# Matmul chains issued in turns into two PSUM banks, in an fp32r attention and MLP kernel

## The reference, cut to what matters

```
for layer in (1, 2):
    h = layer_norm(x)
    q, k, v = h @ wq + bq, ctx @ wk + bk, ctx @ wv + bv      # 16 heads of 128
    k, v = concat(k, bias_k), concat(v, bias_v)              # one more key
    x = x + softmax(q @ k.T / sqrt(128)) @ v @ wo + bo
x = x + gelu(layer_norm(x) @ w_fc1 + b_fc1) @ w_fc2 + b_fc2  # width 2048
```

## Time and profile before

| | us |
|---|---|
| median of 3 runs (lowest, highest) | 2818.55 (2814.38, 2820.99) |
| profiled execution: span from the first to the last instruction | 2818.2 |
| PE busy | 2611.6 (93%) |
| PE weight loads busy | 2209.9 |
| DVE busy | 1351.1 (48%) |
| POOL busy | 910.3 (32%) |
| ACT busy | 889.7 (32%) |
| chain that ended last: PE | 79% of the span |
| of it, matmuls of line 433 | 61% |
| matmuls, and as many weight loads | 14528 |

### The profile page before, as it was taken

One profiled execution on the slowest core, in us unless ns is written; L12 is line 12 of the kernel. 1 busy time (PEld: TensorE's weight loads), 2 busy tenths in 40 slices (PEclk: granted clock), 3 DMA queues, 4 the chain that ended last, 5 costly groups with the idle time before them and its releaser, 6 DMA issues.

```text
span 2818.2 us, 40994 instructions
## 1 busy us (share of the span) xinstructions
PE 2611.6 (93%) x14528; PEld 2209.9 (78%) x14528; DVE 1351.1 (48%) x2100; ACT 889.7 (32%) x2807; POOL 910.3 (32%) x1004
## 2 busy tenths in 40 slices
PE   7998799999899999889979987999998999998898
PEld 5776688888788888767757666888886888887677
DVE  5657633333634334464466576334336333335544
ACT  5775222222222222211147752222223222222110
POOL 4545422322323223232145453223223232233221
PEclk9999899999999999999989998999999999999999
DMA  4000111011111011111130002011011010111100
GB/s 160 23 8 16 64 38 37 32 50 38 57 38 52 30 37 47 40 33 35 64 125 23 8 16 71 31 37 52 30 38 64 30 52 30 37 52 35 37 30 30
DMA packets 34829, 121.70 MB, mean 43 GB/s; under 512 B 3488, under 2 KB 3744, under 8 KB 33696
## 3 DMA queue, kind: packets, MB, share of 16 engines
q1 hardware_dynamic: 34720, 120.27, 12.1%
HBM read 116.06 MB, written 4.19 MB: 43 GB/s over the span
## 4 chain that ended last, share of the span: by engine, by line
PE 79%; issue 7%; DVE 5%; POOL 5%; ACT 2%; DMA 2%; SPq 0%; DVEq 0%; POOLq 0%; ACTq 0%
PE PS L433 61%; PE PS L627 4%; PE PS L609 4%; PE PS L500 3%; PE PS L479 2%; PE PS L618 2%; PE PS L488 2%; POOL X L302 2%; DMA BO<-in_bo_rows 1%; ACT KZ L764 1%; POOL XN L317 1%; DVE XN L1025 1%; PE PS L523 1%; DVE X L967 1%; DVE HF L1043 1%
## 5 line engine op out<-in xcount | busy, mean ns | idle before, releaser
L433 PE MATMUL PS<-AT,W 128*128 128x512 f32 x2496 | 601.0, 392 | 17.7 <-DVE HF L1043 12.1
L433 PEld LDWEIGHTS PS<-AT,W 128*128 128x128 f32 x2496 | 471.6, 189 | 119.5 <-issue 12.5
L967 DVE TENSOR_TENSOR X<-PS,X 128x512 f32<-128x512 f32 x416 | 284.6, 690 | 357.2 <-PE PS L433 352.7
L433 PE MATMUL PS<-CT,W 128*128 128x512 f32 x1728 | 441.0, 404 | 2.9 <-DVE HF L1043 2.9
L433 PE MATMUL PS<-W,CT 128*128 128x256 f32 (+1 forms) x3264 | 421.5, 291 | 19.7 <-DVE CT L917 12.5
L374 POOL TENSOR_TENSOR PR<-PR,RC 128x512 f32<-128x512 f32 x128 | 133.5, 1043 | 935.5 <-DVE RC L1134 935.5
L433 PEld LDWEIGHTS PS<-W,CT 128*128 128x128 f32 x3264 | 410.6, 199 | 20.7 <-issue 12.4
L433 PE MATMUL PS<-W,CX 128*128 128x512 f32 x1584 | 386.8, 399 | 1.5 <-DVE X L967 1.5
L433 PEld LDWEIGHTS PS<-CT,W 128*128 128x128 f32 x1728 | 318.5, 190 | 72.1 <-issue 10.2
L433 PEld LDWEIGHTS PS<-W,CX 128*128 128x128 f32 x1584 | 292.4, 188 | 69.0 <-DVE X L967 3.2
L289 POOL TENSOR_TENSOR W<-RAW,W 128x1024 fp32r<-128x1024 f32 (+1 forms) x136 | 328.6, 2416 | 11.4
(11 more groups left out here) (90 smaller groups left out, 2989.4 us busy)
## 6 DMA issues: line engine op xcount, KB each, us to landing
RAW<-in_wq SPq DMA_DIRECT2D x44, 512.0 KB, 3.3
RAW<-in_wk SPq DMA_DIRECT2D x44, 512.0 KB, 4.2
RAW<-in_wo SPq DMA_DIRECT2D x44, 512.0 KB, 3.3
RAW<-in_wv SPq DMA_DIRECT2D x40, 512.0 KB, 3.3
X<-in_x SPq DMA_DIRECT2D x2, 2048.0 KB, 10.2
BVR<-in_bv_rows SPq DMA_DIRECT2D x8, 512.0 KB, 4.1
BIASVR<-in_biasv_rows SPq DMA_DIRECT2D x8, 512.0 KB, 5.8
out<-X SPq DMA_DIRECT2D x4, 1024.0 KB, 4.3
```

The lines of the kernel that those rows point to most:

```text
L433: ins = nc.tensor.matmul(out, lhs(c, a), rhs(c, b), start=(k == 0), stop=(k == total - 1))
L967: V_.tensor_tensor(X[:, tile, :], PS[:, bank, :], X[:, tile, :], ALU.add).then_inc(done, 1)
```

## The change

Where a chain does not have to wait for its moving operand chunk by chunk (fresh), two chains are issued in turns: one matmul of the first, one of the second. This is done for keys and queries of a head, for the values of a block (a tile of bank BC with a tile of bank BD) and for the two column blocks of hidden(m). The waits of both chains stand ahead of the pair, and both semaphores are raised by the last two matmuls. The number, the shapes and the operands of the matmuls stay as they are, and the other engines' programs are untouched. Chains stay one behind the other for head 0 of a layer's first two blocks and for hidden(0) and hidden(2) of a half's first pair.

```diff
+            def two_chains(first, second, chunks):
+
+                k, total = 0, chunks * len(PASSES)
+                for c in range(chunks):
+                    for a, b in PASSES:
+                        flags = dict(start=(k == 0), stop=(k == total - 1))
+                        one = nc.tensor.matmul(first[0], first[1](c, a), first[2](c, b), **flags)
+                        two = nc.tensor.matmul(second[0], second[1](c, a), second[2](c, b), **flags)
+                        k += 1
+                return one, two
...
                     def qk(n, tb, h, slab, fresh=None):
                         pe.wait_ge(k_ev, n * 2 + h)
-                        keys(n, tb, h, slab)
+                        if fresh is not None:
+                            keys(n, tb, h, slab)
+                            pe.wait_ge(q_ev, n * 2 + h)
+                            queries(n, tb, h, slab, fresh)
+                            return
                         pe.wait_ge(q_ev, n * 2 + h)
-                        queries(n, tb, h, slab, fresh)
+                        if h == 0:
+                            pe.wait_ge(w_ready[1], slab + 1)
+                            pe.wait_ge(w_ready[0], slab + 1)
+                        k_last, q_last = two_chains((PS[:, BB, :], slab_of(1, h * P), block_of(CT, tb)),
+                                                    (PS[:, BA, :], slab_of(0, h * P), block_of(AT, tb)), C)
+                        k_last.then_inc(k_ps, 1)
+                        q_last.then_inc(q_ps, 1)
 
                     def values(n, tb, slab, first):
...
+                        if first == "layer":
+                            pe.wait_ge(xadd, x_count(hf, n) - 2)
+                        elif not first:
+                            pe.wait_ge(xadd, x_count(hf, n) - 4)
...
+                        for b in range(2):
+                            ends = two_chains(tokens(0, b), tokens(1, b), C)
+                        for ins in ends:
                             ins.then_inc(v_ps, 1)
...
+                        if first and e == 0:
+                            for f in range(2):
+                                if m:
+                                    pe.wait_ge(gelu_done, m0 * 2 + (2 * m + f - 1))
+                                fresh = norm_index(hf, LAYERS) * 8 + tb * C if f == 0 else None
+                                project(BA + f, e, 256, f * P, AT, tb, h_ps, fresh)
+                            return
+                        if m:
+                            pe.wait_ge(gelu_done, m0 * 2 + 2 * m)
+                        elif not first:
+                            pe.wait_ge(gelu_done, m0 * 2)
+                        ends = two_chains((PS[:, BA, :], slab_of(e, 0), block_of(AT, tb)),
+                                          (PS[:, BB, :], slab_of(e, P), block_of(AT, tb)), C)
+                        for ins in ends:
+                            ins.then_inc(h_ps, 1)
```

More of the change, by code:

```diff
@@ L441, in project, with slab_of, block_of @@
                        lambda c, b: src[:, b, c, tb * BTOK:(tb + 1) * BTOK], C, fresh).then_inc(done, 1)
+            def two_chains(first, second, chunks):
[7 more added lines that the diff above has]
+                return one, two
+            def slab_of(kind, col):
+                w = W[:, kind].rearrange("p a (c n) -> p a c n", n=256)
+                return lambda c, a: w[:, a, c, col:col + P]
+            def block_of(src, tb):
+                return lambda c, b: src[:, b, c, tb * BTOK:(tb + 1) * BTOK]
             pe.wait_ge(ld_ident, 16)
@@ L589, in values, with tokens @@
                         pe.wait_ge(w_ready[2], slab + 1)
[L590 to L598, removed]
+                        if first == "layer":
+                            pe.wait_ge(xadd, x_count(hf, n) - 2)
+                        elif not first:
+                            pe.wait_ge(xadd, x_count(hf, n) - 4)
+                        def tokens(i, b):
+                            t = (tb * BT + 2 * i + b) * P
+                            return (PS[:, BC + i, b * 256:(b + 1) * 256], lambda c, a: CT[:, a, c, t:t + P],
+                                    lambda c, b_: w[:, b_, c, :])
+                        for b in range(2):
+                            ends = two_chains(tokens(0, b), tokens(1, b), C)
+                        for ins in ends:
                             ins.then_inc(v_ps, 1)
```

## The result

The changed kernel takes 2979.01 us (median of 4 runs, 2976.33 to 2987.17), the kernel before 2819.77 us beside it. The ratio is 1.0573, with a 95% interval of 1.0554 to 1.0591: 159 us slower. The profiled execution has a span of 2985.4 us, 167 more than that of before; it was the slowest of the four (2987.17 us), so its rows add up to some 8 us more than the median.

What follows compares the result with a forecast made beforehand. PE was taken to bound the kernel, busy 386.00 of 386 us in the attention loop, so any wait there is new time. 81 + 2 + 31 + 25 + 6 = 145, and 2818 + 145 = 2963 us, range 2870 to 3010.

Steps and rivals of the forecast that it cites:

- part 1: Distance between matmuls issued in turns: bank turns cost 0; bounds 86 us gained at most, about 18 us lost.
- The third rival: Chain's own bank costs 13 ns per matmul, turns gain 86 us: 2877 with stalls (0.04), 2777 without the collision (0.03).
- part 2: Values: the second DVE eviction of 0.69 us fits into DVE's idle 1.02 us before CX, cost 0.
- part 3: Keys and queries: late K eviction makes DVE's and POOL's splits collide; 28 stalls of 2.88 us, 81 us, plus 2.
- part 4: MLP: hidden(1) waits for both gelus, and additions come later behind both splits; 31 us.
- part 5: Granted clock falling behind waits: 25 us for 28 attention stalls (bounds 0, 46), 6 us in the MLP (0, 9).
- The first rival: Attention, behind late keys: DVE's cast goes before POOL's copy, stall 1.0 us, 29 us in all: 2886; chance 0.10.
- The second: Attention, behind late keys: DVE's and POOL's splits do not block each other, stall 0.2 us: 2863; chance 0.05.

Runs made afterwards that it cites:

- the values alone: Changed kernel with only the values issued in turns; keys, queries and hidden steps one chain behind the other as before: 2819.73 us, ratio 1.0005.
- the MLP alone: Changed kernel with only the MLP's hidden steps issued in turns; keys, queries and values one chain behind the other: 2853.03 us, ratio 1.0132.
- the filled stall: Changed kernel plus 11 matmuls with discarded results put into each of the 28 stalls: 2937.39 us, ratio 1.0418.
- POOL behind DVE: Changed kernel, but POOL starts its splits of a pass only when DVE has split the keys: 2863.83 us, ratio 1.0162.
- keys and queries alone: Changed kernel with only keys and queries issued in turns; values and hidden steps one chain behind the other: 2942.62 us, ratio 1.0440.
- all but one place: Changed kernel, but keys and queries of head 1 in a pass's second block stay one behind the other: 2857.48 us, ratio 1.0145.

## Why the prediction was right, and where it was off

The forecast was 2963 us with a range of 2870 to 3010, and the median is 2979.

- **The pace (part 1).** Costed at 0, and right: 0.227 us from start to start in turns with 512 columns, and no change for the values alone. The third rival, a gain of pace, is out.
- **Values (part 2).** 0 forecast, 1.8 us measured, inside the interval around no change. The 44 us that the prediction worked out from the rule of the Trainium skill (Perfetto Trace Analysis, Matmuls) did not come; the idle time in the row decided. In the MLP, where DVE had no idle time, the same loss of overlap did cost.
- **Keys and queries (part 3).** The sequence came as written: cast blocked, POOL's subtraction next, DVE's subtraction last. From the last query matmul to the end of DVE's subtraction the forecast had 669.87 - 664.32 = 5.55 us and the trace has 695.29 - 689.70 = 5.59. The stall is 2.82 us (forecast 2.88; its terms, 669.87 + 0.69 + 0.04 - 667.74, make 2.86), in 28 passes 79 us (81). In a layer's last pass PE's idle time ahead of the third row tile grew from 0.37 to 0.63 us, 1 us in all (2).
- **The MLP (part 4) with its clock.** 31 + 6 forecast, 35 measured for the MLP alone. The wait of hidden(1) for a gelu, the additions that come late, and the second split behind the blocked first are all in the trace. The 6 us of clock are not confirmed by that sum. By the prediction's own way of reckoning, the clock of 0.97 over two loops of 182 us loses 11 us with the MLP alone, 2 more than before; the 0.93 of the changed kernel's profile, in both loops, loses 25, 17 more, over the upper bound of 9. So agreement to 2 us is in part luck of the runs.
- **The clock behind the stalls (part 5)** is the term that was mis-sized. I took 0.9 us per stall, 25 us, between bounds of 0 and 46. The granted clock fell in every one of the 28 passes, and the filled stall puts it at 42 us, 1.5 for each and close to the upper bound; that is 17 us more than was taken, where forecast and median differ by 16. The step that failed was to scale the 0.7 us per wait of before with the length of the wait. Behind idle times of 2.19 to 2.26 us the clock fell at 5 waits of 12, and behind those of 2.60 to 2.63 us at 28 of 28. What makes it fall is not shown to be the length alone (see the last section).

The first rival (DVE gets its turn first) lost by 0.19 us, as the rows had it. The second, no blocking, is what the kernel with POOL behind DVE measures: 2863.83 against the 2863 written for it.

## What to carry to other kernels

Ask of a chain that ends later not only who waits for its result, but what is queued behind its eviction on the same engine, and which other engine's work that will now meet. Here 0.7 us of eviction, moved by 2.5 us, cost 124 us, because two weight splits that used to run one behind the other now waited for each other. A stall on PE of 2.6 us can be paid a second time behind it through the clock, and a row with a stretched operation (2.73 where 0.69 is usual) is worth a semaphore: one on POOL made the kernel before 1.2% faster.

## What the runs showed of the hardware

- A DVE cast or subtraction with all operands in SBUF and a POOL operation on SBUF wait each other out: 1.41 us for a cast of 0.68, and 3.28 for a subtraction of 1.23. DVE's operations that read PSUM (additions of 0.69, evictions of 0.75) kept their times beside POOL. POOL is stretched as well: its copy took 2.03 us beside DVE's subtraction and 1.05 alone. This agrees with the Trainium skill (SBUF — State Buffer, Who interferes with whom), by which a DVE instruction with two SBUF inputs contends with a GpSimd instruction that reads SBUF, and a DVE cast can do so in a 2-port mode, in which whoever issues first gets the shared pair of ports for the whole instruction. No row tells the mode of a cast.
- The length of one idle time does not settle whether the clock falls behind it. Idle times of 2.60 to 2.63 us were followed by 1.2 GHz in all 28 passes of the changed kernel and in 27 of 28 with keys and queries alone; those of 2.19 to 2.26 us in the MLP of before in 5 of 12. But the MLP's waits of 3.25 to 3.33 us, ten in each kernel, were followed by it in 10 of 10 in the changed kernel and in only 28 of 40 in four others (the MLP alone, all but one place, POOL behind DVE, the filled stall). In the last of these, 26 matmuls behind 3.25 us of idle time run through at the distance of the higher level, (6.33 - 0.39) / 25 = 0.238 us. The 28 stalls are no independent cases either, as they follow each other at 57.9 us within a layer. What decides stays open here.

```profile
1295.85 6.33 PE L433 MATMUL PS<-W,HB 128*128 128x512 f32 x26 [3.25 <-DVE X L1012]
```

- Consecutive fp32r matmuls with 512 columns start 0.227 us apart, whether they add into one bank or alternate between two; those with 256 columns start 0.120 us apart either way.
